# A chunked delta rule on one core: solve's inputs prepared one round ahead, its result copied one round later

## What is computed

```
def step(state, inp):
    q_t, k_t, v_t, a_t, b_t = inp
    state = a_t[..., None, None] * state
    stored = jnp.einsum('bhij,bhj->bhi', state, k_t)
    delta = b_t[..., None] * (v_t - stored)
    state = state + jnp.einsum('bhi,bhj->bhij', delta, k_t)
    o_t = jnp.einsum('bhij,bhj->bhi', state, q_t)
    return (state, o_t)
```

## Time and profile before

| what | value |
| --- | --- |
| median of 3 runs | 4258.26 us (4246.33 to 4261.27) |
| profiled execution | 4248.59 us |
| its span | 4246.8 us |
| busy in the span: PE, DVE, ACT, POOL | 2704.9, 2322.1, 1252.7, 540.7 us |
| mean granted TensorE clock | 0.732 of full speed |
| chunk stage | 62 to 909 us of the span |

### The profile page before, as it was taken

One profiled execution on the slowest core, in us unless ns is written; L12 is line 12 of the kernel. 1 busy time (PEld: TensorE's weight loads), 2 busy tenths in 40 slices (PEclk: granted clock), 3 DMA queues, 4 the chain that ended last, 5 costly groups with the idle time before them and its releaser, 6 DMA issues. The chain is left out here.

```text
span 4246.8 us, 92348 instructions
## 1 busy us (share of the span) xinstructions
PE 2704.9 (64%) x34652; PEld 1931.6 (45%) x34652; DVE 2322.1 (55%) x5466; ACT 1252.7 (29%) x3057; POOL 540.7 (13%) x613
## 2 busy tenths in 40 slices
PE   5986774348888556663367638777775009999900
PEld 2554543335555333331263425555553008999800
DVE  2386564736666488885610337677676204444466
ACT  3764453226666311101200004344332002222200
POOL 0221121100000010000000001101100460000075
PEclk8997886555555578886657559888896559999955
DMA  2546565643333643302039571122111432222255
GB/s 99 191 148 228 198 228 213 214 159 100 103 104 100 173 121 109 99 3 95 13 128 415 219 277 53 52 65 66 52 57 36 161 100 68 70 69 71 73 167 183
DMA packets 412769, 539.30 MB, mean 127 GB/s; under 512 B 177732, under 2 KB 341472, under 8 KB 403168
## 3 DMA queue, kind: packets, MB, share of 16 engines
q1 hardware_dynamic: 361600, 382.34, 28.0%
q0 software_dynamic: 39616, 127.22, 8.3%
q10 hardware_dynamic: 11296, 26.22, 1.6%
HBM read 330.64 MB, written 216.15 MB: 129 GB/s over the span
## 5 line engine op out<-in xcount | busy, mean ns | idle before, releaser
L1021 ACT ACTIVATE ss_write_ps<-ss_state,ss_gammas 128x64 f32<-128x64 f32 x1024 | 263.3, 303 | 195.4 <-DVE ss_state L1069 195.4
L443 PE MATMUL dc_rows_ps<-dc_weights,dc_hT 128*128 128x512 f32 x512 | 290.0, 695 | 8.7 <-issue 5.6
L1193 PE MATMUL do_late_ps<-do_scratch,do_ident 128*128 128x512 f32 (+1 forms) x416 | 197.4, 632 | 109.5 <-DVE do_scratch L1228 109.4
L2459 PE MATMUL se_up_ps<-se_xT,se_w 128*128 128x128 f32 x2176 | 266.6, 276 | 0.1
L500 PE MATMUL dc_solve_ps<-dc_sides,dc_blocks 32*32 32x32 f32 x8192 | 123.5, 226 | 214.2 <-ACT dc_blocks L594 99.8
L2467 PE MATMUL se_y_ps<-se_w,se_aT 128*128 128x256 f32 x1088 | 257.2, 379 | 0.0
L2459 PEld LDWEIGHTS se_up_ps<-se_xT,se_w 128*128 128x128 f32 x2176 | 255.1, 193 | 0.6 <-issue 0.5
L2524 DVE COPY se_w<-mx_weights 128x2048 f32 x136 | 166.7, 1227 | 101.1 <-issue 101.1
L500 PEld LDWEIGHTS dc_solve_ps<-dc_sides,dc_blocks 32*32 32x32 f32 x8192 | 110.9, 139 | 227.7 <-ACT dc_blocks L594 116.6
L2595 POOL DMA_INDIRECT cb_y<-scratch_ys,cb_to x128 | 138.8, 1085 | 589.5 <-DVE cb_to L2610 551.0
L2467 PEld LDWEIGHTS se_y_ps<-se_w,se_aT 128*128 128x128 f32 x1088 | 196.4, 190 | 21.1
(11 more groups left out here) (337 smaller groups left out, 5806.9 us busy)
## 6 DMA issues: line engine op xcount, KB each, us to landing
ex_w<-in_w_all SPq DMA_DIRECT2D x64, 1024.0 KB, 21.7
scratch_rows<-dc_rows POOLq DMA_DIRECT2D x64, 512.0 KB, 4.2
scratch_vw<-dc_out POOLq DMA_DIRECT2D x64, 512.0 KB, 4.5
dc_c_rows<-scratch_rows SPq DMA_DIRECT2D x64, 384.0 KB, 4.5
scratch_xs<-wa_zeros ACTq DMA_DIRECT2D x34, 512.0 KB, 14.1
se_xs<-scratch_xs SPq DMA_DIRECT2D x136, 128.0 KB, 2.0
scratch_ys<-se_y SPq DMA_DIRECT2D x136, 128.0 KB
ss_wq_rows<-scratch_vw SPq DMA_DIRECT2D x128, 128.0 KB, 2.2
```

Of the source, the lines that this page charges most:

```text
L443: mm = pe.matmul(to, hT[n % 2][:, k, :], weights[:, k, columns], start=(k == 0), stop=(k == HALVES - 1), skip_group_check=True)
L1021: ins = act.activation(write_ps[b][:, k, 0:WIDTH], state[b][:, k, :], ACT.Copy, scale=gammas[i][:, b, k, c:c + 1])
L1193: mm = pe.matmul(late_ps[:, to:to + (2 - skip) * DIM], ident[:, :], scratch[lag % 2][:, (t + skip - lag) * DIM:(t + 2 - lag) * DIM], start ...
L2459: mm = pe.matmul(up_ps[i % 2][:, c * P:(c + 1) * P], w[i % (2 * AHEAD)][:, k * DFF + c * P:k * DFF + (c + 1) * P], xT[i % 2][:, k, :], sta ...
```

## The change

ACT makes the blocks of the next tile in the middle of a round and copies the result of the tile solved in the round before near the beginning. DVE scales the next tile's rows, and this and `normalize` move ahead of `select` and `sum_squares`. `out` gets a third buffer, with waits for the tile three back.

```
-        out = [sb(f"out{i}", [P, 4 * DIM]) for i in both]
+        out = [sb(f"out{i}", [P, 4 * DIM]) for i in range(3)]
...
                 def copy_vw(c):
                     act.wait_ge(tile_solved, at(c + 1))
-                    if c >= 2:
-                        act.wait_ge(out_done[c % 2], 16 * (c // 2))
-                    act.copy(out[c % 2][:, 0:2 * DIM], solve_ps[:, :]).then_inc(vw_copied, 1)
+                    if c >= 3:
+                        act.wait_ge(out_done[c % 3], 16 * (c // 3))
+                    act.copy(out[c % 3][:, 0:2 * DIM], solve_ps[:, :]).then_inc(vw_copied, 1)
...
                         root(n // LN + 1)
+                    c = n - C_LAG
+                    if 0 <= c - 1 < TILES:
+                        copy_vw(c - 1)
                     if n >= 4 and n % 2 == 0 and n - 4 < TILES:
                         take_first_half((n - 4) // 2)
                     if n < TILES:
                         copy_vk(n)
                         copy_ab(n)
+                    if 0 <= c + 1 < TILES:
+                        make_blocks(c + 1)
                     if 0 <= n - 1 < TILES:
                         copy_qkT(n - 1)
...
-                    if 0 <= c < TILES:
-                        make_blocks(c)
-                        copy_vw(c)
...
-                    if c >= 2:
-                        vec.wait_ge(out_done[c % 2], 16 * (c // 2))
+                    if c >= 3:
+                        vec.wait_ge(out_done[c % 3], 16 * (c // 3))
...
                         measure(n // LN + 1)
+                    if n % LN == 2 and n // LN + 1 < TILES // LN:
+                        normalize(n // LN + 1)
+                    c = n - C_LAG + 1
+                    if 0 <= c < TILES:
+                        scale_tile(c)
                     if n >= 4 and n % 2 == 0 and n - 4 < TILES:
                         select((n - 4) // 2)
                     if 0 <= n - 1 < TILES:
                         sum_squares(n - 1)
-                    if n % LN == 2 and n // LN + 1 < TILES // LN:
-                        normalize(n // LN + 1)
-                    c = n - C_LAG
-                    if 0 <= c < TILES:
-                        scale_tile(c)
```

More of the change, by code:

```diff
@@ L319, in build_delta_chunks @@
         blocks_ready, sides_ready, scaled, tile_solved, vw_copied = map(sem, ("blocks_ready", "sides_ready", "scaled", "tile_solved", "vw_copied"))
-        out_done = [sem.from_zero(f"out_done{i}") for i in both]
+        out_done = [sem.from_zero(f"out_done{i}") for i in range(3)]
         CONSTS = 16 * (5 + 4 * BATCH)
@@ L419, in _ @@
                         pool.wait_ge(vw_copied, at(c + 1))
-                        pool.dma_start(tile_rows(d["vw"], c), out[c % 2][:, :]).then_inc(out_done[c % 2], 16)
-                for i in both:
-                    pool.wait_ge(out_done[i], 16 * TILES // 2)
+                        pool.dma_start(tile_rows(d["vw"], c), out[c % 3][:, :]).then_inc(out_done[c % 3], 16)
+                for i in range(3):
+                    pool.wait_ge(out_done[i], 16 * ((TILES + 2 - i) // 3))
                 pool.wait_ge(qkd_out, 16 * GROUPS)
@@ L688, in scale_tile @@
                                       ALU.mult).then_inc(sides_ready, 1)
-                    if c >= 2:
-                        vec.wait_ge(out_done[c % 2], 16 * (c // 2))
-                    vec.tensor_tensor(heads(out[c % 2][:, 2 * DIM:4 * DIM]), heads(c_rows[c % 3][:, K:K + 2 * DIM]), spread(c_fac[c % 3][:, 2 * HEADS:4 * HEADS], HEAD),
+                    if c >= 3:
+                        vec.wait_ge(out_done[c % 3], 16 * (c // 3))
+                    vec.tensor_tensor(heads(out[c % 3][:, 2 * DIM:4 * DIM]), heads(c_rows[c % 3][:, K:K + 2 * DIM]), spread(c_fac[c % 3][:, 2 * HEADS:4 * HEADS], HEAD),
                                       ALU.mult).then_inc(scaled, 1)
```

## The result

The changed kernel takes 4294.78 us (median of 3 runs, 4288.53 to 4298.1) against 4258.26: a ratio of 1.0091, 95% interval 1.0055 to 1.0126. The profiled execution took 4294.78 us as well, its span 4293.0; the span before was 4246.8. This difference, 46.2 us, is what the two traces can account for. It is 10 us more than that of the medians, since the profiled execution before lay 10 us under its median. The chunk stage makes 45.2 of the 46.2 us.

A forecast was written before the change was run, and what follows sets the result against it. It took instruction packets to bound the solves and a load-store chain the group edges. Terms -5 + 0 + 1.6 + 13 + 15 + 6 = +31 us gave 4279 us profiled, 4289 median; range 4248 to 4308.

The forecast's parts named there:

- the signs that it named: Right if solves' issue stops rise from 33.2 to 45 us or more, DVE idles 8 to 10 us before early scalings.
- Packets: PE in the solves: instructions come in packets of about 256, each asked for when the previous begins; 4.5 us.
- Rival 1: Solves: the next packet is fetched ahead, so the blocks' waits are gained; -10 us, 4249; chance 0.13.
- Rivals 2 and 3: 2: edges cost nothing, blocks' waits gained, 4213 us; 3: edges bounded by bytes, solves by packets, 4253; chance 0.13 each.
- Blocks ahead: PE's waits for blocks go, mostly exchanged for longer stops; four or five solves gain, -5 us in full rounds.
- in the full rounds [...] nothing: Scalings ahead on DVE: it idles 6.4 us per wait ahead of select, against 1.4 + 1.7 put in front; nothing.
- First edge +13, second +15: Rounds 35-37 and 51-54: early scaling delays the queries' weighing and the pair loads; +13 (6 to 18), +15 (8 to 20).
- Third edge +6, fourth 0: After projecting ends: tile 32's scaling delays the weighing, +6 us (3 to 9); fourth hidden in DVE's store wait, 0.
- Last tiles 0: Last 13 tiles: packets every 4.81 us hide the shorter loop; 0, bounds -19.5 and +4 if traffic slows packets.
- Third buffer 0: Rows that leave: DVE's scaling waits for the same store, only copy_vw is freed, at the edges; 0.
- Round 26, +1.6: Round 26: DVE is late and PE waits for select, which comes 1.7 us later; +1.6 us.
- ScalarE's blocks ahead of copies, "nothing": ACT: blocks now precede the copies of qkT and qg, but pair products and solve on PE come first; nothing.

The follow-up runs named there:

- Run 11: Kernel before the change with the last 13 tiles' solves issued twice; ratio 1.0132 against before, +56 us.
- run 1: ScalarE's part of the change with the third out buffer, VectorE's order as before the change; ratio 1.0029 against before, +12 us.
- run 6: Kernel before the change with a fourth buffer for tile inputs, so that SP loads a tile's rows earlier; ratio 1.0050 against before, +21 us.
- run 5: Changed kernel with SP's load of a tile held until the solve of the tile three back has ended; ratio 1.0067 against before, +28 us.
- run 3: Changed kernel with the next tile's scaling last in VectorE's round; ratio 0.9988 against before, -5 us.
- run 12: Changed kernel with tile 16g+1's load ahead of the group's key products, query products loaded two rounds later; ratio 1.0040 against before, +17 us.
- run 8: Kernel before the change with the third out buffer alone; ratio 0.9991 against before.
- run 7: Changed kernel with scaling last in VectorE's round and the load held until the solve three tiles back ended; ratio 0.9977 against before, -10 us.
- 9: Changed kernel with scaling last, load held, and ScalarE's blocks of the next tile last in its round; ratio 0.9965 against before, -15 us.

## Why the prediction was right, and where it was not

The total was right: slower, 4289 forecast and 4294.8 measured. The sum behind it was +31 us for the profiled execution, which grew by 46. Its main mechanism, the first two edges, was right, but that the total came so near is luck: the full rounds took 26.7 us more than forecast, the first 36 rounds and the drain 12.4 less, and the medians differ by 10 less than the profiled executions. Of the signs that it named, DVE's idle time ahead of the early scaling came (11.49 and 12.09 us), and the stops inside the solves from round 37 to 62 rose from 33.2 to 67.3 us, far past the 45 asked for.

- **Packets.** Right. Run 11 shows two packets a tile at 4.4 us each, run 1 the exchange of waits for stops. Rival 1, by which packets run ahead, has fallen: the stops grew when the waits went. The Trainium skill's "mostly hidden" (page "Runtime: NRT & Kernel Launch", section "Instruction fetch mechanics") does not hold in these solves, where PE stopped in all 14 from round 37 on, for 38.3 us. Rivals 2 and 3, by which the edges cost nothing, have fallen with the edges. One reading in the working was loose: the records hold 548 instructions a round, which leaves 36 over two packets, while the stop's moving by 21 matmuls asks for 42.
- **Blocks ahead, -5 in the full rounds.** The step that failed, together with "in the full rounds [...] nothing" for the scalings. For each part alone the forecast was close (+1.5 and +2.3 from round 37 to 51). What I did not count was SP's load: it waits for the later of blocks and scaling, and when both move a round ahead, 384 KB of rows go out just as the packet is asked for. Measured by moving the load alone: +10.7 us (run 6) and -13.3 us (run 5) in 14 rounds; run 3 lost 11.7 us there with few early loads, so it is not the only way to lose them. The forecast spoke of DMA traffic only as a risk for the last tiles. The 4.5 us of a packet was read off one round and taken as fixed.
- **First edge +13, second +15.** Right: +14.6 and +13.7. VectorE's part alone does it (+15.1, +13.3), the scaling put last undoes it at the first edge and two thirds of it at the second (28.3 and 47.8 us), and with tile 16g+1's load freed of the queries' store (run 12) most of it goes at both.
- **Third edge +6, fourth 0.** Together +6 for the drain, measured +0.2. The third edge itself came as forecast: the solve of tile 33 follows that of tile 32 by 29.5 us instead of 22.6, +6.9. From tile 47 to 48, at the fourth, it was 13.9 instead of 9.5, +4.4 where 0 stood. The rest of the drain became 11.1 us shorter, against "makes nothing good". The two parts have opposite signs there: ScalarE's alone gave -11.2 for the whole drain, VectorE's +4.4. The first I had at 0. Part of it may be the third buffer (run 8: -7.6, in one profile); that was not separated further.
- **Last tiles 0.** Right: stops took the place of the wait, and the 59.5 us from tile 51 on did not change.
- **Third buffer 0.** Right in the total (run 8).
- **Round 26, +1.6.** Wrong in sign: the first 36 rounds gained 5.0 us. I only priced what stands behind the normalization, not that PE may get its next four tiles sooner by it. That this is the way is argued, and no total shows the gain.
- **ScalarE's blocks ahead of copies, "nothing".** Wrong at the second edge: with the scaling in its old place ACT stood 16.9 us there and the stretch grew by 7.8 (run 1); that the first made the second was not tested in that kernel. In the change itself it does not show: at the first edge PE waits 7.55 us for ACT's copy (L571) in round 36, and then 20.77 us for DVE all the same.

Three things stay open: what bounds the second edge at 46 to 48 us in runs 3, 7 and 9, where it took 42.9 before (the stop in round 51 makes 2.4 to 2.6 us of it); what else than the load lengthens the full rounds of run 3, and so why the hold gained less in run 7 than in run 5; and whether the load delays the packet by its own bytes or by the stores of POOL that then meet it.

## What to carry over

Work moved ahead in its engine's order releases whatever waits for it, here a DMA load, so ask where that lands as well as what the move removes; a wait on two semaphores moves fully only when both do, and here one-at-a-time tests of the change missed it (+1.5 and +2.3 us, together +13.0). At a boundary where a load must wait for a store, nothing that needs the load may stand ahead of what feeds the store, and the small load that is needed now belongs ahead of the large ones needed rounds later, which with scaling and blocks last gave 4228 us against 4253.

## What the runs showed of the hardware that was not expected

An instruction packet's time is not fixed. Of the 14 packets that the changed kernel asks for during the pair products of rounds 37 to 50, the seven with a load of 384 KB issued 1.2 to 0.2 us ahead took 5.15 us in the mean and the other seven 3.39; with the load held back, the same seven took 3.86, as before the change (3.87). The share of busy DMA in all was no larger (0.44 against 0.50 before). And a stop can cost more than itself. Here is run 1's timeline of PE behind a stop of 4.68 us and behind one of 2.28:

```profile
344.73 0.54 PE L500 MATMUL dc_solve_ps<-dc_sides,dc_blocks 32*32 32x32 f32 x22 [4.68 <-issue]
345.20 0.69 PE L438 MATMUL dc_t_ps<-dc_ident,dc_x 128*128 128x128 f32 x2
345.68 3.62 PE L443 MATMUL dc_rows_ps<-dc_weights,dc_hT 128*128 128x512 f32 x4
...
357.94 0.57 PE L500 MATMUL dc_solve_ps<-dc_sides,dc_blocks 32*32 32x32 f32 x42 [2.28 <-issue]
358.44 0.44 PE L438 MATMUL dc_t_ps<-dc_ident,dc_x 128*128 128x128 f32 x2
358.72 1.88 PE L443 MATMUL dc_rows_ps<-dc_weights,dc_hT 128*128 128x512 f32 x4
```

The same four matmuls take 3.62 us at 1.2 GHz and 1.88 at 2.4 GHz. In the window behind the changed kernel's stop of 4.44 us the granted clock was 0.56:

```profile
380.30:384.60 4.30, 4.30 (x22) 2.25 (x13) 3.92 (x13) 1.50 (x4) 1.07 (x2) 0.56 0.06 18
```

So a stop can be followed by work at the lower clock, and in the change 23.0 us of longer stops stand beside 4.3 us of longer busy time. How much of the 4.3 follows from the stops is not shown: run 1 had 29.9 us of stops, twice those of before, and was busy for 3.1 us less. The length of the stop alone does not tell it either: round 38 before, with a stop of only 1.37 us, was followed by four such matmuls at 3.62 us.
